# Expert 1's second layer in high and low parts with features by tokens, x's moments on ScalarE, and VectorE's second half in another order

## The reference

```python
xn = _layernorm(x, axis=-1)
x = x + attention(xn) + experts(xn)
...
logits = einsum('bsh,he->bse', xn, router_w) + router_b + load_balancer
rw, sel = jax.lax.top_k(logits, 2); rw = softmax(rw)
e0 = silu(xn @ sw_w1) * (xn @ sw_w3) @ sw_w2
sym = ((xn @ me_eq_w + me_eq_b) @ me_wv + me_bv) @ me_wo + me_bo
e1 = gelu(sym @ me_c1w + me_c1b) @ me_c2w + me_c2b
...                                  # e2: two layer norms and a relu layer
e3 = gelu(xn @ ml_w1 + ml_b1) @ ml_w2 + ml_b2
out = (rw[..., None] * gathered).sum(axis=2)
```

## Time and profile before

| | |
|---|---|
| median of three runs | 442.15 us (441.63 to 442.38) |
| the profiled execution | 441.77 us, of which the profiled span is 439.8 |
| TensorE, VectorE, GpSimd, ScalarE busy | 97%, 88%, 75%, 63% of the span |
| granted TensorE clock | 1.0 |
| DMA | 35.03 MB, 34% of the 16 engines' time |

### The profile page before, as it was taken

The page is one execution under the profiler, slowest core; times in us unless marked ns, Lnnn a source line. Parts: engine busy times, 40 slices in busy tenths (PEclk is TensorE's granted clock), DMA queues, the critical chain, the costliest instruction groups (busy, mean ns, idle before and its releaser), DMA issues.

```text
span 439.8 us, 9655 instructions
## 1 busy us (share of the span) xinstructions
PE 427.9 (97%) x2760; PEld 364.6 (83%) x2760; DVE 387.3 (88%) x1229; ACT 275.5 (63%) x534; POOL 328.4 (75%) x478
## 2 busy tenths in 40 slices
PE   4989999999999999999999999999999999999996
PEld 4768888888888888888788888888888888888876
DVE  4886898998999899898998999899899989988887
ACT  4874847568385665838567484756838566583851
POOL 3897596886859778695986859688685977868394
PEclk9999999999999999999999999999999999999999
DMA  7533324243251523424143242423325152341301
GB/s 261 44 73 82 64 74 95 49 102 73 73 110 40 132 48 89 78 72 102 41 113 77 75 92 72 95 48 100 72 70 113 37 135 48 88 79 50 72 1 48
DMA packets 120322, 35.03 MB, mean 80 GB/s; under 512 B 96912, under 2 KB 114032, under 8 KB 120304
## 3 DMA queue, kind: packets, MB, share of 16 engines
q1 hardware_dynamic: 120016, 34.80, 33.6%
q10 hardware_dynamic: 288, 0.01, 0.0%
HBM read 18.60 MB, written 15.99 MB: 79 GB/s over the span
## 4 chain that ended last, share of the span: by engine, by line
PE 95%; DVE 2%; DMA 1%; ACT 1%; issue 0%; DVEq 0%; SPq 0%
PE S L1179 15%; PE S L1181 13%; PE S L1180 13%; PE EX L1103 12%; PE EX L1123 6%; PE S L1273 3%; PE S L1278 3%; PE S L1274 3%; PE EX L1133 3%; PE S L1286 2%; PE S L1284 2%; PE S L1285 2%; PE S L1194 2%; PE S L1193 2%; PE S L1192 2%; PE TR L1221 1%
## 5 line engine op out<-in xcount | busy, mean ns | idle before, releaser
L503 POOL TENSOR_TENSOR hid3l<-hid,hid3h 128x512 fp32r<-128x512 f32 x64 | 80.7, 1293 | 59.8 <-ACT hid3h L647 59.8
L1179 PE MATMUL S<-xh,WH 128*128 128x512 f32 x224 | 91.7, 409 | 0.0
L1181 PE MATMUL S<-xh,WL 128*128 128x512 f32 x224 | 88.3, 394 | 0.0
L1180 PE MATMUL S<-xl,WH 128*128 128x512 f32 x224 | 88.3, 394 | 0.0
L1103 PEld LDWEIGHTS EX<-scaled,hid 128*128 128x128 f32 x480 | 55.9, 192 | 1.2
L1103 PE MATMUL EX<-scaled,hid 128*128 128x128 f32 x480 | 56.0, 275 | 0.0
L803 DVE SCALAR_TENSOR_TENSOR OUT<-EX,coef,OUT 128x128 f32<-128x128 f32 x184 | 51.6, 343 | 1.0
L1181 PEld LDWEIGHTS S<-xh,WL 128*128 128x128 f32 x224 | 42.1, 188 | 10.1
L568 ACT CAST xh<-TR 128x512 fp32r<-128x512 f32 x16 | 9.4, 587 | 64.0 <-DVE TR L860 64.0
L1179 PEld LDWEIGHTS S<-xh,WH 128*128 128x128 f32 x224 | 42.1, 188 | 8.5
L1180 PEld LDWEIGHTS S<-xl,WH 128*128 128x128 f32 x224 | 42.3, 189 | 7.9
(11 more groups left out here) (199 smaller groups left out, 1066.7 us busy)
## 6 DMA issues: line engine op xcount, KB each, us to landing
X<-x SPq DMA_DIRECT2D x16, 256.0 KB, 2.9
turning<-xn SPq DMA_DIRECT2D x15, 256.0 KB, 2.4
xb<-turning SPq DMA_DIRECT2D x60, 64.0 KB, 2.6
turning<-e3T SPq DMA_DIRECT2D x15, 256.0 KB, 2.1
turning<-u SPq DMA_DIRECT2D x15, 256.0 KB, 2.3
e3b<-turning SPq DMA_DIRECT2D x60, 64.0 KB, 2.7
ub<-turning SPq DMA_DIRECT2D x60, 64.0 KB, 2.6
out<-OUT SPq DMA_DIRECT2D x15, 256.0 KB, 2.3
```

Of the source, the lines that this page charges most:

```text
L503: pool.tensor_tensor(hid3l[:, j, :], hid[3][:, j, :], hid3h[:, j, :], ALU.subtract) \
L1179: pe.matmul(bank[:, :], wh, hi, start=True, stop=False)
L1180: pe.matmul(bank[:, :], wh, lo, start=False, stop=False)
L1181: pe.matmul(bank[:, :], wl, hi, start=False, stop=True).then_inc(unit_ready, 1)
```

## The change

1. Expert 1's second layer: its weights get high and low parts (`c2`, split with the third block of weights), and so does its hidden layer: `hid1h` on ScalarE at the turn's end, `hid1l` on GpSimd. `expert1` on TensorE becomes six `F32R` products of 512 columns, with features by tokens as the result. ScalarE adds the bias (`lay_e1`, into `e1T`), SyncE writes and reads back (`keep_e1`, `swap_e1`), VectorE transposes and mixes (`sum_expert1`). The bias `me_c2b` leaves GpSimd's `add_biases`, except in the last turn. The last group's expert 1 keeps its old form.
2. X's moments go from VectorE to ScalarE: four sums and four sums of squares with the activation's accumulated output. GpSimd's norm of x goes from the end of a turn to the next turn's start, behind the norm of c (`norm_spread_x`). Turns 0 and 1 keep VectorE's moments for their own x.
3. VectorE's second half: the transpose of u goes ahead of `foundl`, u's moments right behind it, then `OUT`, then the route; `sum_expert1` stands behind `silu(3)`.

```diff
-WEIGHT_SPLITS = [(SPLIT["w1"], "sw_w1", 2 * I), (SPLIT["ml"], "ml_w1", I + 2 * P), (SPLIT["f2"], "f2w", 2 * P + I)]
+WEIGHT_SPLITS = [(SPLIT["w1"], "sw_w1", 2 * I), (SPLIT["ml"], "ml_w1", I + 2 * P), (SPLIT["f2"], "f2w", 2 * P + I + 2 * P)]
...
+            at, _ = ROWS["me_c2b"]
+            sp.dma_start(c2_bias[:, :], bass.AP(rows.tensor, rows.offset + at, [[1, P], [1, 1]])) \
+                .then_inc(c2_bias_loaded, DMA_INC)
...
-            def swap_x(g):
+            def keep_x(g):
                 sp.wait_ge(x_normed, g.count(NT, NT))
                 sp.dma_start(turning[0], xn[:, :, :]).then_inc(x_kept, DMA_INC)
+
+            def keep_e1(g):
+                sp.wait_ge(e1_laid, g.count(1, 1))
+                sp.dma_start(turning[3], e1T[:, :, :]).then_inc(e1_kept, DMA_INC)
+
+            def swap_e1(g):
+                sp.wait_ge(e1_kept, g.count(DMA_INC, DMA_INC))
+                swap_back(e1b, turning[3], e1_swapped)
...
                 if not last:
+                    keep_x(g.next())
+                if not first:
+                    keep_e1(g.prev())
+                if not last:
                     swap_x(g.next())
+                if not first:
+                    swap_e1(g.prev())
                 if two_more(g):
                     sp.wait_ge(att_added, g.count(1, 1))
                     load_x(Group(g.pair, g.off + 2))
...
+            def norm_spread_x(g):
+
+                pool.wait_ge(x_stats, g.count(1, 1))
+                pool.tensor_tensor(veps["x"][:, :], spread[:, :], share[:, :], ALU.mult)
...
                     norm_x(g.next())
+                elif not last:
+                    norm_spread_x(g.next())
...
-                add_biases(g, first)
-                if two_more(g):
-                    norm_x(Group(g.pair, g.off + 2))
+                if last:
+                    add_biases(g)
+                else:
+                    add_bias2(g, first)
+                    pool.wait_ge(hid1_high, g.count(1, 1))
+                    pool.tensor_tensor(hid1l[:, :, :], hid[1][:, :, :], hid1h[:, :, :], ALU.subtract) \
+                        .then_inc(hid1_low, 1)
...
+                if not first:
+                    lay_e1(g.prev())
                 act.wait_ge(found_ready, g.count(1, 1))
                 act.copy(foundh[:, :], ATT[:, 0, :]).then_inc(found_taken, 1)
...
+                half_gate(3)
                 act.wait_ge(lean_ready, g.count(1, 1))
                 act.activation(tlean[:, :, :], lean[:, :, :], ACT.Tanh).then_inc(tlean_ready, 1)
-                half_gate(3)
+                if two_more(g):
+                    x_moments(Group(g.pair, g.off + 2))
                 if not last:
                     take_x(g.next())
...
+                if not last:
+                    act.wait_ge(released[g.bank("m1")], g.uses_before("m1") + 1)
+                    act.copy(hid1h[:, :, :], hid[1][:, :, :]).then_inc(hid1_high, 1)
+
+            def lay_e1(g):
+
+                act.wait_ge(c2_bias_loaded, DMA_INC)
+                wait(act, e1_kept, g.count(DMA_INC, 0))
+                act.wait_ge(ex_ready[1], g.count(1, 1))
+                act.activation(e1T[:, :, :], EX[EX_BANK[1]][:, :, :], ACT.Identity, bias=c2_bias[:, :]).then_inc(e1_laid, 1)
+
+            def x_moments(g):
+
+                act.wait_ge(x_normed, g.prev().count(NT, NT))
+                act.wait_ge(x_loaded[g.par], g.half(DMA_INC, DMA_INC))
+                for t in range(NT):
+                    act.activation(xsq[:, t, :], X[g.par][:, t, :], ACT.Identity, scale=-1.0 / P,
+                                   accum_out=negmean["x"][:, t:t + 1]).then_inc(x_mean, 1)
+                act.wait_ge(x_mean, Group(g.pair, g.off - 2).count(NT, NT))
+                for t in range(NT):
+                    ins = act.activation(xsq[:, t, :], X[g.par][:, t, :], ACT.Square, bias=negmean["x"][:, t:t + 1],
+                                         accum_out=spread[:, t:t + 1])
+                ins.then_inc(x_stats, 1)
...
+            def sum_expert1(g):
+
+                dve.wait_ge(e1_swapped, g.count(SWAPS * DMA_INC, SWAPS * DMA_INC))
+                dve.wait_ge(ex_taken[0], g.count(1, 1))
+                dve.transpose(EX[EX_BANK[1]][:, :, :].rearrange("p t n -> p (t n)"),
+                              e1b[:, :, :].rearrange("p t n -> p (t n)")).then_inc(e1_turned, 1)
...
                 if not first:
-                    expert1(g.prev())
+                    turn_u(g.prev())
                 found_rest(g)
+                if not first:
+                    u_moments(g.prev())
+                    u_combine(g.prev())
...
                 silu(3)
+                if not first:
+                    sum_expert1(g.prev())
                 if not last:
                     turn_next(g)
...
-                if two_more(g):
-                    x_moments(Group(g.pair, g.off + 2))
...
                 pe.wait_ge(ex_taken[0], g.count(1, 1))
-                b = g.bank("m1")
-                pe.wait_ge(released[b], g.uses_before("m1") + 1)
-                for t in range(NT):
-                    for j in range(2):
-                        ins = pe.matmul(EX[EX_BANK[1]][:, t, :], hid[1][:, j, t * P:(t + 1) * P],
-                                        w("me_c2w", j * P, P), start=(j == 0), stop=(j == 1))
+                pe.wait_ge(hid1_low, g.count(1, 1))
+                bank = EX[EX_BANK[1]][:, :, :].rearrange("p t n -> p (t n)")
+                for j in range(2):
+                    wh, wl = (m[:, SPLIT["c2"] + j * P:SPLIT["c2"] + (j + 1) * P] for m in (WH, WL))
+                    pe.matmul(bank, wh, hid1h[:, j, :], start=(j == 0), stop=False)
+                    pe.matmul(bank, wl, hid1h[:, j, :], start=False, stop=False)
+                for j in range(2):
+                    wh = WH[:, SPLIT["c2"] + j * P:SPLIT["c2"] + (j + 1) * P]
+                    ins = pe.matmul(bank, wh, hid1l[:, j, :], start=False, stop=(j == 1))
```

More of the change, by code:

```diff
@@ L204, in build @@
         rstd = {k: sb(f"rstd_{k}", [P, NT]) for k in "xcu"}
+        xsq = sb("xsq", [P, NT, P])
+        spread = sb("spread", [P, NT])
+        share = sb("share", [P, NT])
+        hid1h = sb("hid1h", [P, 2, T], F32R)
+        hid1l = sb("hid1l", [P, 2, T], F32R)
+        e1T = sb("e1T", [P, NT, P])
+        e1b = sb("e1b", [P, NT, P])
+        c2_bias = sb("c2_bias", [P, 1])
         more = sb("more", [P, NT, E, E])
@@ L471, in norm, with scale @@
                 pool.drain()
+                scale(k, src, dst, done)
+            def scale(k, src, dst, done):
                 for t in range(NT):
@@ L945, in turn @@
                 if not first:
-                    expert1(g.prev())
+                    turn_u(g.prev())
                 found_rest(g)
+                if not first:
+                    u_moments(g.prev())
+                    u_combine(g.prev())
+                wait(dve, out_stored[g.par], g.half(DMA_INC, 0))
+                dve.wait_ge(att_ready, g.count(1, 1))
+                dve.tensor_tensor(OUT[g.par][:, :, :], ATT[:, :, :], X[g.par][:, :, :], ALU.add) \
+                    .then_inc(att_added, 1)
                 route(dve.tensor_copy(again, logit))
```

55 lines of the change are left out of this document (39 added, 16 removed).

## The result

| | before | after |
|---|---|---|
| median of the runs | 442.38 us (441.63 to 444.36) | 466.58 us (466.11 to 467.22) |
| ratio to before, with its interval | | 1.0542 (1.0517 to 1.0566) |
| profiled span | 439.8 us | 465.4 us |
| TensorE, VectorE, GpSimd, ScalarE busy | 97, 88, 75, 63% | 93, 82, 71, 71% |
| mean turn, 1 to 13 | 26.12 us | 27.87 us |

The forecast was 459.9 us with a range of 446 to 476. One run of the experiments (moments_vector, 478.33 us at a granted clock of 0.855) was in a slower state of the chip and is left out of all figures.

What follows compares the result with a forecast made beforehand. TensorE bounds the kernel before; a closed chain through X's load and ScalarE's moments sets turns 1 to 13 after. 441.77 + 16.6 + 0.3 + 0.7 + 0.1 = 459.5, plus 0.4 for the median: 459.9 us, range 446 to 476.

Steps and rivals of the forecast that it cites:

- the ring: From `kv` over `e1T`, SyncE's queue, X and ScalarE's moments to the next `kv`: 27.4 us, 1.28 more in turns 1 to 13.
- The marks named for it: Profile after: turns about 27.4 us, ScalarE's first moment waiting for X, TensorE waiting 1 us or more at the first gate product.
- issue of X to the first moment: SyncE's load of X, from issue to landing, ahead of ScalarE's moments: 2.9 us.
- eight moments: X's four means at 0.285 and four squares at 0.400 on ScalarE, without overlap: 2.7 us.
- hand-offs: Six or so passes from engine to engine in the turn's closed chain: 0.2 us allowed together.
- The wait for `found`: TensorE waits 0.48 us a turn because `e1T` precedes `foundh` on ScalarE, eating the products' saving: net +0.04.
- Expert 1's products: On TensorE, six products of 512 columns take 0.44 us less a turn; the step back may take up to 0.1.
- Just in time, 0.1 at most: Expert 0 waits for VectorE to take expert 1, at 22.0 us behind `kv`, when TensorE wants it: 0.1 at most.
- the ring is not the longest: Rival: X lands before ScalarE reaches the moments, TensorE sets the turn; +2.2, 444 us; chance 0.11.
- faster: Rival: TensorE stays the only bound and keeps 0.44 us a turn; 436.3 us; chance 0.05.
- Start, turn 0 and tail: Start 0.1 us for more columns and a load; turn 0 loads X as before; tail 0.7 with the short waits.
- GpSimd and VectorE's order: GpSimd's moved norm and low part of `hid1`, and VectorE's new order, are hidden: costed at nothing.

Runs made afterwards that it cites:

- moments_vector: Against the kernel after: X's moments back on VectorE at their old place, GpSimd's norm taken from them; 465.82 us, ratio 1.0543.
- load_early: Against the kernel after: SyncE loads X ahead of expert 1's four pieces, not behind them; 456.93 us, ratio 1.0308.
- squares_twice: Against the kernel after: ScalarE does the four squares of the moments a second time into scratch; 495.72 us, ratio 1.118.
- found_first: Against bank_freed: ScalarE lays `e1T` behind `foundh`, not ahead of it; 447.91 us, ratio 1.01.
- bank_freed: Against load_early: expert 1 transposed into SBUF, expert 0 waits for `e1_laid` only, x's transpose and expert 2's mix ahead of expert 1's; 448.63 us, ratio 1.0115.
- e1_late: Against found_first: `e1T` behind `th2`, its write behind x's pieces, expert 3 turned earlier, expert 1 mixed last, `hid1l` behind, groups 14 and 15 plain; 438.05 us.
- moments_alone: Against the kernel before: only X's moments on ScalarE and GpSimd's norm of x behind the norm of c; 442.70 us, ratio 1.0002.
- order_alone: Against the kernel before: only VectorE's new order, expert 1's mix in its old form; 443.03 us, ratio 0.999.

## Why the prediction was right, step by step

**The bound, the sign and the mechanism** were as forecast, and load_early, squares_twice and the absence of any wait of `kv` for TensorE show the ring, not only the number. The marks named for it are in the trace: the wait of the first moment for X, no other hole ahead of `xh` and `kv`, TensorE's wait at the first gate product for `pl`. Only that last one is smaller than named, 0.7 us a turn and 1.0 at most in place of 1 or more, since a part of the ring's excess waits at expert 0. The ring's terms, mean of turns 1 to 13:

| term | forecast | after |
|---|---|---|
| `kv` to the issue of X | 18.26 | 18.56 |
| issue of X to the first moment | 2.9 | 3.15 |
| eight moments | 2.7 | 2.87 |
| `xh` to `hid1h` | 2.33 | 2.33 |
| `hid1h` to `kv` | 1.05 | 0.96 |
| hand-offs, forecast in one | 0.2 | in the rows |
| turn | 27.4 | 27.87 |

**What was mis-sized** is small in each term and adds up to 0.47 a turn, 6.1 us over 13 turns; the start, turns 0 and 14 and the tail add 1.9. The profiled execution, 467.2 us, is 7.7 above the sum of 459.5. The medians are 6.7 apart only, since this one came out 0.6 below the profiled execution and not 0.4 above it; that part is luck. X is issued 0.3 later than the sum, of which 0.21 is a gap between expert 1's last piece (ends 228.47) and X (228.68); for all hand-offs together I had allowed 0.2. From its issue to the first moment are 0.25 more: the page of after gives X's landing as 3.2 us against the 2.9 of the earlier trace rows. With the same eight pieces ahead it is 3.0 in moments_vector, and in load_early it is 3.3 with four, so their number is not the reason; which is, stays open. The moments were taken at the 0.285 and 0.400 of the earlier trace rows, and their steps are 0.29 and 0.39, but the step from the last mean to the first square is 0.42.

**The wait for `found`** was put at 0.48 with a net of +0.04 a turn. The table has +0.42 and -0.39, a net of +0.03. found_first shows both apart, since it removes the one and keeps the other.

**Expert 1's products** were put at 0.44 fewer, less up to 0.1 for the step back: 0.39.

**"Just in time, 0.1 at most"** for expert 0's bank was wrong. The tile's last piece takes 2.96 us to land on average, not 2.6, so expert 1's transpose starts at 20.66 behind `kv` where the sum has 20.2. TensorE's stretch up to expert 0 is 0.51 us longer in the kernel after (3.30 against 2.79), and 0.78 in load_early, where X no longer holds the turn. In the kernel after this cost nothing more, as `kv` never waited for TensorE. It was the failed step for anything beyond: I looked at expert 1's way through DRAM as a wait of one product, and did not see that VectorE's order hangs behind it with the transpose of x, and so forms a second limit of 27.1 us a turn (load_early), and of 27.8 with the moments on VectorE (moments_vector).

**The rival "the ring is not the longest", 444 us,** had neither the right condition nor the right remainder. In load_early the way to X was 2.8 us shorter and the time was 457, because of that second limit; it took bank_freed as well to reach 448.6. And X need not land before ScalarE reaches the moments: in e1_late ScalarE still waits 30.8 us for X in all, and the turn is 25.83. Its 5.0 us of new work for ScalarE is 4.4 by the prediction's own terms (`e1T`, moments, `hid1h`).

**The rival "faster"** was priced at 436.3 and tied to `e1T` ahead of `foundh` costing 0.1 at most and a ring below 25.7. Both can be had by moving work: e1_late, with the same products in all groups but two, is at 438.05.

**Start, turn 0 and tail** were put at 0.1, 0 and 0.7 and took 0.29, 0.87 and 1.5. In turn 0 X is issued 18.6 us behind `kv` against 16.4 before. The order is the forecast one, but SyncE could issue x's pieces only 3.8 us behind the write of xn (26.16 to 29.95), where it was 2.1 us before (25.37 to 27.43) and 2.0 in load_early, whose turn 0 has the same instructions and takes 27.69. So some 0.8 of the 0.87 is a write that landed late in this execution; found_first and e1_late have it too. What the tail's 1.5 are was not taken apart; with the plain form for group 14 and the other edits of e1_late it is 32.75.

**GpSimd and VectorE's order** were costed at nothing, and nothing is what moments_alone and order_alone show for the norm's new place and the new order. GpSimd's `hid1l` is in neither; e1_late, which has it, is not held up by it.

## What to carry to other kernels

When a load is queued behind DMAs that need this turn's results, and an in-order engine waits for it ahead of work that starts the next turn, the turn is a ring; add up its rows from one start to the same start a turn later, and then look for what limits the turn next, since here a limit of about 27.1 us lay under the ring of 27.9 (27.11 in load_early, where expert 1's tile lands 0.3 later), and shortening the ring by 2.8 gave 0.8. Where a product is replaced by a cheaper one with a longer way home, place the copies of that way behind everything that TensorE waits for soon, and let its result land in memory that no product needs. The last one or two turns of a loop can keep the old form, since there a longer way home is not hidden.

## What the runs showed of the hardware that I had not expected

- **The clock.** In squares_twice TensorE fell to the lower level in five turns, for some 3.4 us each (0.43 us a product, granted clock 0.81 over 9 us), every time at the second of two waits of 0.9 to 1.4 and about 1.0 us that end 2.6 us apart. In turns 9 and 10 two such waits (1.42 and 0.97, 1.27 and 0.96) left it at the upper level, and so did waits of up to 1.1 us in the kernel after. So in a kernel with a ring a little more length can cost more than itself, here 1.3 to 1.8 us in each of the turns 11 to 13.
- **A mix that reads two SBUF tiles beside GpSimd.** In found_first the longest of them took 2.51 us instead of 0.34, ending 0.14 us behind GpSimd's `hid1l`; the one that had started 0.17 us ahead of `hid1l` took 0.35. With `hid1l` placed behind it (e1_late) four take 1.14. The rows show the coincidence in turns 14 and 15, and that it is gone; no run has only that edit. The Trainium skill ("SBUF — State Buffer", Who interferes with whom) says that a VectorE instruction with two SBUF inputs contends with a GpSimd instruction that reads SBUF; the trace agrees. With its tile in PSUM, as in the kernel after, 57 of the 60 instructions of that mix ran beside one of GpSimd's, and the longest took 0.35 us.
- **The accumulator's read-out** is an instruction of its own, 0.19 us behind each accumulated activation, with some 0.1 of it ahead of the next one's start.
